# Row maxima of attention scores by a relu of a score difference: 22 tiles ahead of the loop, one tile in four inside it

## The chip, the cores and the metric

The program runs on 1 core of one Trainium2 chip. A core has a matrix engine (TensorE, PE in the rows; PEld is its weight load), a vector engine (VectorE, DVE), a scalar engine (ScalarE, ACT), GpSimd (POOL), a queue engine (SyncE, SP) and 16 DMA engines. Each engine works through its own list of instructions in order, and semaphores order the engines among each other. The metric is device time in microseconds (us), the median over runs; lower is better.

## The reference, cut to what matters

The program computes two layers on x of shape 2 x 1024 x 256: grouped attention with rotary positions, a feed-forward block with table-coded weights, a recurrent time-mix layer and a mixture of experts. The change touches the attention of the first layer:

```python
q = compute_rope((x @ W_Q.T).reshape(2, 1024, 16, 16))     # 16 heads of 16 numbers
k = compute_rope((x @ W_K.T).reshape(2, 1024, 16, 8))      # 8 key heads, each for 2 query heads
scores = einsum('bsdkg,btdk->bkgst', q, k) / sqrt(256)
w = softmax(scores, axis=-1)
ctx = einsum('bkgst,btdk->bkgsd', w, v)
```

The softmax needs the maximum of each query row over its 1024 keys before the exponentials can be taken. Feed-forward weights are `lut[idx]`, sixteen table values looked up by index; that lookup is done by other engines while attention runs.

## The kernel before, in words

**Projection.** The first 55 us load x, normalize it, turn it, and compute q, k and v on PE for four blocks of 512 tokens. DVE applies the rotary positions (`rope`), ACT cuts the result into a high part (`cut`), POOL makes the low part (`low_parts`), and SP stores both to DRAM (`block_out`); from there `load_qk` brings them back as tiles QS and KS with 48 rows per head (three products of 16 numbers), the two query heads of a key head at partitions 0 and 64. The pair of batch and key head is called n (0 to 15).

**Row maxima.** For one n there are 16 tiles of 128 queries (8 query blocks, 2 heads g). For tile k PE makes two matmuls (`maximum(k, 0)` and `maximum(k, 1)`, line 765), each 128 queries by 512 keys into a bank of PSUM, and DVE reduces the 128 x 1024 scores to 128 maxima (`row_max`, line 695). Two pairs of banks take turns, so the matmul of tile k waits for the reduction of tile k-2 (`max_done`). After 16 tiles the maxima are turned (`turn_max`), split in two parts by POOL (`max_parts`), sent through DRAM and loaded as two more rows of QS (`place_max`), so that the score matmul subtracts them. The first 26 tiles (16 + AHEAD) are made ahead of the loop.

**The loop.** For each n there are 8 steps t. PE's list in a step is, in this order: the two matmuls of tile k (k = 26 + 16n + 2t); the scores S0 and S1 (line 781, 128 keys by 512 queries each); four matmuls with the values for step t-2 (`weigh`, line 793, each shown as two records); the scores S2 and S3; the two matmuls of tile k+1. Scores go to a ring of three banks, so a score waits until the exponential three places before it has left its bank (`p_ready`). ACT takes the exponentials E0 to E3 of a step in order (line 681), and once per n it copies the result out (line 563) between E2 and E3 of step 1. DVE's list in a step is the reductions of k and k+1, and in even steps a table lookup between them (line 720), whose products POOL adds (line 622). In the last rounds the lookups come closer together.

The order is written out by hand in the functions `attend_tensor`, `attend_scalar`, `attend_vector`, `attend_gpsimd` and `attend_sync`; nothing is scheduled by a tool.

## Time and profile before

| | |
|---|---|
| device time, median of 3 runs | 884.34 us (880.03 to 892.65) |
| span of the profiled execution | 864.7 us |
| median less the span | 19.6 us (lowest run less the span: 15.3) |
| PE busy | 780.4 us, 90% |
| DVE busy | 694.2 us, 80% |
| ACT busy | 524.5 us, 61% |
| POOL busy | 363.9 us, 42% |

The busy times are sums over the whole program, whose stages have different limits; what the change is worth has to be read from the two stages it touches: about 56 to 89 us (tiles ahead of the loop) and 89 to 438 us (the loop). The pace of a stage shows in the distance of starts in the timeline, and what bounds it in the wait that ends last.

### The profile page before, as it was taken

The numbers are of one execution on the slowest core, as the hardware profiler recorded it, in microseconds if no ns is written. First come the engines' busy times: TensorE is split into PE (matmuls) and PEld (weight loads), VectorE is DVE, ScalarE is ACT, GpSimd is POOL, SyncE is SP. The second block draws the span as 40 slices with busy tenths as digits, with TensorE's granted clock in tenths as the row PEclk, the third lists the DMA queues.
The fourth block names the chain that finished last, engine by engine and source line by source line (L and its number), as shares of the span: only waits on it lengthen the run. The fifth ranks groups of instructions, "written<-read, shape, count | busy, mean of one in ns | idle before, by whom it ended". The sixth has DMA issues, their size and how long they took to land. (4 is left out here: it accounts for less than half of the span.)

```text
span 864.7 us, 17911 instructions
## 1 busy us (share of the span) xinstructions
PE 780.4 (90%) x6593; PEld 503.9 (58%) x6593; DVE 694.2 (80%) x1094; ACT 524.5 (61%) x965; POOL 363.9 (42%) x296
## 2 busy tenths in 40 slices
PE   3999999999999999998999999899575989999996
PEld 2863333333333333332368888798465887999875
DVE  5789999999999999996137666567899877666586
ACT  4520688888788888886864333543757653666442
POOL 6430255535753575359410001003698680444340
PEclk9985799999999999997999999999587989999999
DMA  6497022222222222200029000000104423344352
GB/s 240 174 225 290 2 46 54 52 52 52 52 53 52 52 52 52 56 16 13 20 85 250 2 1 0 14 1 13 60 5 150 174 93 60 117 131 127 115 160 74
DMA packets 59510, 69.97 MB, mean 81 GB/s; under 512 B 24768, under 2 KB 46400, under 8 KB 59040
## 3 DMA queue, kind: packets, MB, share of 16 engines
q1 hardware_dynamic: 55272, 58.30, 24.9%
q0 software_dynamic: 3408, 9.38, 3.1%
q10 hardware_dynamic: 744, 1.15, 0.4%
q8 instruction: 54, 0.88, 0.4%
q14 instruction: 32, 0.26, 0.1%
HBM read 40.07 MB, written 26.62 MB: 77 GB/s over the span
## 5 line engine op out<-in xcount | busy, mean ns | idle before, releaser
L681 ACT ACTIVATE probs_t<-psum 128x512 f32<-128x512 f32 x512 | 271.6, 601 | 98.7 <-PE psum L781 96.7
L695 DVE TENSOR_REDUCE row_max<-psum 128x1 f32<-128x1024 f32 x256 | 297.7, 1213 | 6.2 <-PE psum L765 5.9
L622 POOL TENSOR_TENSOR lut_sum<-lut_sum,lut_tmp 128x1080 f32<-128x1080 f32 x60 | 151.8, 2530 | 160.6 <-DVE lut_tmp L720 159.9
L765 PE MATMUL psum<-KS,QS 48*128 48x512 f32 x512 | 188.7, 470 | 19.6 <-DVE row_max L695 18.6
L781 PE MATMUL psum<-QS,KS 50*128 50x512 f32 x512 | 194.7, 471 | 1.0 <-ACT probs_t L681 1.0
L781 PEld LDWEIGHTS psum<-QS,KS 50*128 50x128 f32 x512 | 82.9, 189 | 135.3 <-ACT probs_t L681 124.7
L793 PE MATMUL psum<-probs_t,VS 128*32 128x512 f32 x1024 | 139.1, 616 | 1.0
L765 PEld LDWEIGHTS psum<-KS,QS 48*128 48x128 f32 x512 | 81.3, 199 | 76.1 <-DVE row_max L695 70.9
L2420 POOL DMA_INDIRECT y_rows<-y_slot,ids x39 | 37.5, 961 | 62.4 <-ACT y_slot L2483 62.1
L720 DVE TENSOR_SCALAR lut_tmp<-lut_idx,lut 128x1080 f32<-128x1080 int32 x60 | 48.7, 813 | 10.2 <-POOL lut_sum L622 10.2
L1179 POOL TENSOR_TENSOR rstd<-var_eps,minus_half 128x4 f32<-128x4 f32 x8 | 8.4, 1044 | 100.5 <-DVE var_eps L1174 100.5
L793 PEld LDWEIGHTS psum<-probs_t,VS 128*32 128x32 f32 x1024 | 20.8, 108 | 37.1 <-ACT probs_t L681 24.8
L1277 POOL TENSOR_TENSOR key<-key,tot 128x512 f32<-128x512 f32 x24 | 29.6, 1251 | 9.5 <-PE psum L2184 7.3
L450 PE MATMUL psum<-xTh,ffn_l 128*128 128x512 f32 (+1 forms) x80 | 31.5, 394 | 1.4 <-DVE f_h L1039 1.4
L452 PE MATMUL psum<-xTh,ffn_h 128*128 128x512 f32 (+1 forms) x80 | 31.5, 393 | 0.0
L451 PE MATMUL psum<-xTl,ffn_h 128*128 128x512 f32 (+1 forms) x80 | 31.5, 393 | 0.0
L984 ACT ACTIVATE f_silu<-psum 128x512 f32<-128x512 f32 (+1 forms) x24 | 14.3, 597 | 27.9 <-PE psum L452 27.9
L2579 DVE TENSOR_TENSOR xt_l<-psum,xt_h 128x256 fp32r<-128x256 f32 x39 | 16.5, 424 | 17.6 <-ACT xt_h L2490 17.5
L991 ACT ACTIVATE f_hh<-f_h 128x512 fp32r<-128x512 f32 (+1 forms) x24 | 15.2, 631 | 23.8 <-DVE f_h L1039 23.0
L1039 DVE TENSOR_TENSOR f_h<-psum,f_silu 128x512 f32<-128x512 f32 (+1 forms) x24 | 16.5, 687 | 16.0 <-ACT f_silu L984 15.6
L2483 ACT ACTIVATE y_slot<-psum,w_tile 128x256 f32<-128x256 f32 x39 | 18.6, 476 | 16.6 <-PE psum L2736 16.6
L2184 PE MATMUL psum<-recept,key 128*32 128x64 f32 x1024 | 21.0, 244 | 7.6 <-issue 4.5
(322 smaller groups left out, 1801.9 us busy)
## 6 DMA issues: line engine op xcount, KB each, us to landing
KS<-k_rows SPq DMA_DIRECT2D x31, 192.0 KB, 4.6
QS<-q_rows SPq DMA_DIRECT2D x31, 192.0 KB, 4.9
x_rows<-zero_rows SPq DMA_DIRECT2D x1, 4992.0 KB, 17.8
x_slot<-x_rows SPq DMA_DIRECT2D x39, 128.0 KB, 2.2
m_raw<-experts_w SPq DMA_DIRECT2D x2, 2432.0 KB, 13.3
q_rows<-part SPq DMA_DIRECT2D x8, 512.0 KB, 8.7
y_token<-y_rows SPq DMA_DIRECT2D x8, 512.0 KB, 7.6
x_tok<-x SPq DMA_DIRECT2D x4, 512.0 KB, 7.4
```

The source lines that it names most:

```text
L450: nc.tensor.matmul(out, ll, rh, start=start and i == 0, stop=False)
L451: nc.tensor.matmul(out, lh, rl, start=False, stop=False)
L452: mm = nc.tensor.matmul(out, lh, rh, start=False, stop=stop and i == n - 1)
L622: nc.gpsimd.tensor_tensor(wsum[:, c % 2, :], wsum[:, c % 2, :], wtmp[:, slot % 2, :], ALU.add).then_inc(lut_add, 1)
L681: nc.scalar.activation(pt[:, k % NPT, :], ring(k)[:], ACT.Exp, scale=float(E) ** -0.5).then_inc(p_ready, 1)
L695: nc.vector.tensor_reduce(mx[:, n % 2, col:col + 1], m.psum[:, 2 * (k % 2):2 * (k % 2) + 2, :], AX_XY, ALU.max).then_inc(max_done, 1)
L720: nc.vector.tensor_scalar(wsum[:, c % 2, :] if v == 0 else wtmp[:, slot % 2, :], idx[:, cols], float(v), lut[:, v:v + 1], ALU.is_equal, AL ...
L765: mm = nc.tensor.matmul(MX[k % 2][h][:], QS[n % NQK][rows(g, NROW), st * P:(st + 1) * P], KS[n % NQK][rows(g, NROW), h * BLK:(h + 1) * BLK ...
L781: nc.tensor.matmul(ring(k)[:], KS[n % NQK][rows(g, NAUG), t * P:(t + 1) * P], QS[n % NQK][rows(g, NAUG), half * BLK:(half + 1) * BLK], sta ...
L793: nc.tensor.matmul(OB[32 * j:32 * (j + 1), :], m.VS[:, bb * NTT + t, kv, :], pt[:, k % NPT, :], start=(t == 0), stop=(t == NTT - 1)).then_ ...
L1277: nc.gpsimd.tensor_tensor(k[:, :, 0, :], k[:, :, 0, :], t[:, :, 1].unsqueeze(2).broadcast_to([P, S // (2 * s), s]), ALU.mult).then_inc(k_d ...
L2420: nc.gpsimd.indirect_dma_start(m.y_rows, bass.IndirectOffsetOnAxis(ap=ids[:, j:j + 1], axis=0), yo[:, j % 4, :], None).then_inc(ys_out[j % ...
```

## The change

For keys in two halves, max(a, b) = relu(a - b) + b. A tile by the new way is: PE makes the score *difference* (queries against the difference of the two halves of the keys, tile KD) into the first bank and the scores of the second half into the second bank; ACT takes the relu of the first bank to SBUF (128 x 512); DVE does one `tensor_tensor_reduce` over 128 x 512: relu plus second bank, reduced by max. ACT's relu waits for both matmuls of the tile (`max_ps`).

- Ahead of the loop: tiles 0 to 3 as before, tiles 4 to 25 (22 tiles) the new way; all eight banks serve as four pairs, so a matmul waits for the reduction four tiles back.
- In the loop: tiles with k % 4 == 3 from 27 to 255 (58 tiles) the new way. These are tile k+1 of the even steps. ACT's relu stands between E1 and E2 of that step. Two pairs of banks, as before.
- The key difference: POOL subtracts the halves (`difference`), ACT and POOL split it, SP stores it to DRAM (`kd_rows`), and `load_diff` loads it per n, on ACT's queue for n = 0, else on SP's.
- SP's list at the start is in another order: the difference goes out ahead of the loads of QS and KS; the stores of the second half of q and k, and the load for n = 3, now follow behind `place_max(0)`, which has moved from ACT's queue to SP's; the first table index load comes earlier, the second at n = 1.
- Tiles for table sums and lookups have other addresses, and the sum is kept whole.

```diff
+    def difference(pool, bb):
+        pool.wait_ge(rot_ready, 6 * bb + 6)
+        if bb >= 1:
+            pool.wait_ge(kd_out, 32 * bb)
+        nc.gpsimd.tensor_tensor(kd[:], krot[0][:], krot[1][:], ALU.subtract).then_inc(kd_ready, 1)
...
         take_xt(3)
+        difference_high(act, 0)
...
         cut(act, 2)
+        act.wait_ge(kd_out, 32)
+        m.load_diff(act, 0)
         take_v(act, 2)
...
+    FIRST, PLAIN = NST + AHEAD, 4
+    def pair(k):
+        return 2 * (k % 4) if k < FIRST else 2 * (k % 2)
+    def by_relu(k):
+        return PLAIN <= k < FIRST or k % 4 == 3 and k >= FIRST
...
+    def part_above(act, k):
+        act.wait_ge(max_ps, k + 1)
+        if k == PLAIN:
+            act.wait_ge(m.prod_k, 2 * NB)
+        nc.scalar.activation(relus[k % 4 if k < FIRST else 0][:], bank[pair(k)], ACT.Relu).then_inc(relu_done, 1)

     def attend_scalar(act):
         m.project_scalar(act)
-        place_max(act, 0)
+        for k in range(PLAIN, FIRST):
+            part_above(act, k)
+            if k == NST - 1:
+                m.difference_high(act, 1)
...
                 nc.scalar.activation(pt[:, k % NPT, :], ring(k)[:], ACT.Exp,
                                      scale=float(E) ** -0.5).then_inc(p_ready, 1)
+                unit = (n + 1) * NST + AHEAD + G * (i // NJ) + 1
+                if i % NJ == 1 and unit < NG * NST and by_relu(unit):
+                    part_above(act, unit)
...
+            out, j = mx[:, n % 2, col:col + 1], pair(k)
+            if by_relu(k):
+                dve.wait_ge(relu_done, relu_number(k) + 1)
+                above = relus[k % 4 if k < FIRST else 0]
+                nc.vector.tensor_tensor_reduce(above[:], bank[j + 1], above[:], 1.0, LOWEST, ALU.add, ALU.max,
+                                               out).then_inc(max_done, 1)
+            else:
+                nc.vector.tensor_reduce(out, m.psum[:, j:j + 2, :], AX_XY, ALU.max).then_inc(max_done, 1)
...
-            if k >= 2 and h == 0:
-                pe.wait_ge(max_done, k - 1)
+            back = 4 if k < FIRST else 2
+            if k >= back and h == 0:
+                pe.wait_ge(max_done, k - back + 1)
```

SP's list in the change, from the first store of the difference:

```diff
         sp.wait_ge(m.ones_ready, NQK)
+        m.difference_out(sp, 0)
         load_qk(sp, 0, (0,))
-        for n in range(1, NQK):
-            load_qk(sp, n)
-        for tb in range(NB // 2, NB):
-            m.block_out(sp, tb)
...
+        load_qk(sp, 1)
+        sp.wait_ge(m.kd_out, 32)
+        load_diff(sp, 1)
+        load_qk(sp, 2)
...
+        load_diff(sp, 2)
+        place_max(sp, 0)
+        m.difference_out(sp, 1)
+        load_qk(sp, NQK - 1)
+        for tb in range(NB // 2, NB):
+            m.block_out(sp, tb)
         for n in range(NG):
+            if n == 0:
+                place_max(sp, 1)
```

How the instructions stand. ACT's list where the loop begins, before: line 580 and 584 place the first maxima, line 681 is the exponentials, line 563 the copy of the result.

```order
L580 DMA m_rows<-max_parts 16x2x32 x3
L584 DMA QS_72<-m_rows 2x1024 [waits mp_out]
L584 DMA QS_72<-m_rows 2x1024
L681 ACTIVATE probs_t<-psum 128x512 [waits s_ps] x10
L681 ACTIVATE probs_t<-psum 128x512 [waits pv_done,s_ps] x29
L563 ACTIVATE o_sb<-psum 128x512 [waits pv_done]
```

The same place in the change: line 766 is the relu, line 791 the exponentials, line 647 the copy.

```order
L766 ACTIVATE relu_108<-psum 128x512 [waits max_ps]
L766 ACTIVATE relu_109<-psum 128x512 [waits max_ps]
L791 ACTIVATE probs_t<-psum 128x512 [waits s_ps] x2
L766 ACTIVATE relu_108<-psum 128x512 [waits max_ps]
L791 ACTIVATE probs_t<-psum 128x512 [waits s_ps] x8
L766 ACTIVATE relu_108<-psum 128x512 [waits max_ps]
L791 ACTIVATE probs_t<-psum 128x512 [waits pv_done,s_ps] x8
L766 ACTIVATE relu_108<-psum 128x512 [waits max_ps]
L791 ACTIVATE probs_t<-psum 128x512 [waits pv_done,s_ps] x8
```

The relu has come in after two exponentials (E0, E1 of an even step) and then after every eighth; E2 and E3 of that step stand behind it.

PE's list in the change over a step and a half of n = 0: line 909 is the scores, line 921 the matmuls with the values, line 897 those for the maxima; KD2 is the key difference for n = 2.

```order
L909 MATMUL psum<-QS0_72,KS0_76 128x512 [waits p_ready] x2
L921 MATMUL psum<-probs_t_87,VS_55 32x512 [waits p_ready] x4
L909 MATMUL psum<-QS0_72,KS0_76 128x512 [waits p_ready] x2
L897 MATMUL psum<-KD2_105,QS2_74 128x512 [waits kd_in2,max_done]
L897 MATMUL psum<-KS2_78,QS2_74 128x512
L897 MATMUL psum<-KS2_78,QS2_74 128x512 [waits max_done]
L897 MATMUL psum<-KS2_78,QS2_74 128x512
L909 MATMUL psum<-QS0_72,KS0_76 128x512 [waits p_ready] x2
```

The places are those of before (there line 765 with KS stood where KD2 stands now): the matmuls whose result the relu takes come behind S2 and S3 of the step, and S0 and S1 of the next step behind the matmuls of the next tile.

DVE's list in the change, where the lookups in the loop begin: line 813 is the new reduction, one instruction over 128 x 512 and one that writes the 128 maxima; line 816 the old one, line 843 the lookup.

```order
L816 TENSOR_REDUCE row_max<-psum 128x1 [waits max_ps]
L843 TENSOR_SCALAR lut_sum<-lut_idx,lut 128x1080 [waits max_done,idx_in,lut_in]
L813 ISA relu_108,row_max<-psum,relu_108 128x512 [waits relu_done,max_ps]
L813 ISA row_max 128x1
L816 TENSOR_REDUCE row_max<-psum 128x1 [waits max_ps] x3
L843 TENSOR_SCALAR lut_tmp<-lut_idx,lut 128x1080 [waits kd_out]
L813 ISA relu_108,row_max<-psum,relu_108 128x512 [waits relu_done,max_ps]
L813 ISA row_max 128x1
```

Per two steps DVE has three old reductions, one new one (as two instructions) and one lookup; before it had four old ones and the lookup.

## Rows read from the trace of the kernel before

**Rows 1.** The page: costliest groups (count, busy us, mean ns, idle before and releaser).

```profile
L681 ACT ACTIVATE probs_t<-psum 128x512 f32<-128x512 f32 x512 | 271.6, 601 | 98.7 <-PE psum L781 96.7
L695 DVE TENSOR_REDUCE row_max<-psum 128x1 f32<-128x1024 f32 x256 | 297.7, 1213 | 6.2 <-PE psum L765 5.9
...
L720 DVE TENSOR_SCALAR lut_tmp<-lut_idx,lut 128x1080 f32<-128x1080 int32 x60 | 48.7, 813 | 10.2 <-POOL lut_sum L622 10.2
```

**Rows 2.** Windows: start:end length, busy PE, PEld, DVE, ACT, POOL, PEclk, DMA share, GB/s.

```profile
88.90:437.80 348.90, 330.95 (x2008) 118.23 (x2011) 315.61 (x325) 281.31 (x533) 180.26 (x112) 0.97 0.20 42
393.60:409.30 15.70, 13.65 (x60) 4.18 (x56) 9.97 (x12) 8.77 (x17) 13.64 (x9) 0.67 0.06 13
59.60:75.00 15.40, 14.13 (x25) 6.05 (x25) 14.33 (x14) 0.00 (x0) 0.89 (x1) 0.50 1.02 346
```

**Rows 3.** Timeline, PE held up behind a lookup: start, duration, engine, line, idle and releaser.

```profile
303.70 0.50 PE L765 MATMUL psum<-KS,QS 48*128 48x512 f32 x1 [0.29 <-DVE row_max L695]
```

**Rows 4.** Timeline, the loop step after that one (PE and ACT).

```profile
305.43 0.49 PE L781 MATMUL psum<-QS,KS 50*128 50x512 f32 x1
...
305.77 0.69 PE L765 MATMUL psum<-KS,QS 48*128 48x512 f32 x2
...
305.96 2.06 ACT L681 ACTIVATE probs_t<-psum 128x512 f32<-128x512 f32 x4 [0.37 <-PE psum L781]
...
306.61 0.50 PE L781 MATMUL psum<-QS,KS 50*128 50x512 f32 x1
...
308.04 0.49 PE L781 MATMUL psum<-QS,KS 50*128 50x512 f32 x1
```

**Rows 5.** Timeline, steps with no maxima; the second one holds the copy of the result.

```profile
417.15 0.50 PE L781 MATMUL psum<-QS,KS 50*128 50x512 f32 x2
...
419.76 0.50 PE L781 MATMUL psum<-QS,KS 50*128 50x512 f32 x2
...
420.79 0.59 ACT L563 ACTIVATE o_sb<-psum 128x512 f32<-128x512 f32 x1
...
422.52 0.50 PE L781 MATMUL psum<-QS,KS 50*128 50x512 f32 x2
```

**Rows 6.** Timeline in the projection and at the first tiles: DVE, POOL, SP's queue.

```profile
38.75 3.80 POOL L242 TENSOR_TENSOR part<-rotated,part 128x512 fp32r<-128x512 f32 x3 [5.25 <-ACT part L229]
...
40.23 1.29 DVE L370 TENSOR_TENSOR xTl<-psum,xTh 128x512 fp32r<-128x512 f32 x2 [2.07 <-ACT xTh L294]
...
46.38 0.33 SPq L190 DMA_DIRECT2D KS<-k_rows  x1
...
56.12 4.61 DVE L695 TENSOR_REDUCE row_max<-psum 128x1 f32<-128x1024 f32 x4 [2.28 <-PE psum L765]
```

**Rows 7.** Timeline, the last tiles ahead of the loop and the first exponentials.

```profile
85.06 2.35 PE L765 MATMUL psum<-KS,QS 48*128 48x512 f32 x4 [0.18 <-DVE row_max L695]
...
87.59 0.79 PE L765 MATMUL psum<-KS,QS 48*128 48x512 f32 x1 [0.18 <-DVE row_max L695]
...
88.88 2.08 ACT L681 ACTIVATE probs_t<-psum 128x512 f32<-128x512 f32 x4 [31.15 <-PE psum L781]
```

**Rows 8.** DMA issues from 30 to 110 us: count, KB each, median us to landing.

```profile
KS<-k_rows SPq DMA_DIRECT2D x7, 192.0 KB, 8.2
```

**Rows 9.** Timeline at 391 us: who takes a tile as soon as its matmuls end.

```profile
390.99 0.49 PE L781 MATMUL psum<-QS,KS 50*128 50x512 f32 x1
...
391.51 2.06 ACT L681 ACTIVATE probs_t<-psum 128x512 f32<-128x512 f32 x4 [0.37 <-PE psum L781]
...
391.79 1.23 DVE L695 TENSOR_REDUCE row_max<-psum 128x1 f32<-128x1024 f32 x1 [0.33 <-PE psum L765]
```

**Rows 10.** Timeline, a long wait in the loop and the steps behind it.

```profile
396.11 0.49 PE L765 MATMUL psum<-KS,QS 48*128 48x512 f32 x1 [1.79 <-DVE row_max L695]
...
402.12 1.22 PE L781 MATMUL psum<-QS,KS 50*128 50x512 f32 x3
...
406.18 0.79 PE L781 MATMUL psum<-QS,KS 50*128 50x512 f32 x2
```

More of the change, by code:

```diff
@@ L348, in project_gpsimd @@
         nc.gpsimd.memset(m.KS[NQK - 1][:].bitcast(F32), 1.0).then_inc(ones_ready, 1)
-        for tb in range(NB):
-            low_parts(pool, tb)
+        for bb in range(B):
+            for tb in (2 * bb, 2 * bb + 1):
+                low_parts(pool, tb)
+            difference(pool, bb)
+            difference_low(pool, bb)
     def project_vector(dve):
@@ L503, in attention_stage @@
     mres_done = sem("mres_done")
+    relu_done = m.front_sem("relu_done")
+    kd_in = [m.front_sem(f"kd_in{i}") for i in range(4)]
     gu_ps = m.gu_ps = sem("gu_ps")
@@ L758, in maximum @@
                 pe.wait_ge(qk_in[n % NQK], 16 * m.LOADS * (n // NQK + 1))
[L759 to L760 removed]
+            back = 4 if k < FIRST else 2
+            if k >= back and h == 0:
+                pe.wait_ge(max_done, k - back + 1)
             if k == 1 and h == 0:
                 pe.wait_ge(m.v_out, NT)
+            if k == 2 and h == 0:
+                pe.wait_ge(m.prod_q, 4 * NB)
+                pe.wait_ge(m.prod_k, 2 * NB)
             st, g = divmod(i, G)
[L765 to L766 removed]
+            keys = KS[n % NQK][rows(g, NROW), h * BLK:(h + 1) * BLK]
+            if by_relu(k) and h == 0:
+                q = diff_tile(n)
+                pe.wait_ge(kd_in[q], 32 if n < 2 else 16 * (n // 2))
+                keys = KD[q][rows(g, NROW), :]
+            mm = nc.tensor.matmul(bank[pair(k) + h], QS[n % NQK][rows(g, NROW), st * P:(st + 1) * P], keys,
+                                  start=True, stop=True)
             if h == 1:
@@ L817, in up_two @@
                 mm.then_inc(gu_ps, 1)
-        for k in range(NST + AHEAD):
+        for k in range(FIRST):
             maximum(k, 0)
@@ L1193, in norm @@
                                     ALU.subtract, ALU.mult).then_inc(m.xb_ready, 1)
+LOWEST = -3.4028234663852886e38
 LH, LD = 4, 64
```

110 lines of the change are left out of this document (80 added, 30 removed).

## The prediction

> **What bounds the kernel now.** I read the page's groups first. DVE spends 297.7 us on 256 reductions of 1.21 us, and ACT, with 512 exponentials, idles 98.7 us, nearly all of it waiting for PE's scores [rows 1]. The windows show where: over the loop (348.9 us for 128 steps, so 2.73 us a step) DVE is busy 315.6, ACT 281.3 and PE 331 us; ahead of it, at 59.6 to 75 us, DVE is busy 14.3 of 15.4 us, ACT not at all, and PE runs at a granted clock of 0.50, its 1.2 GHz level [rows 2].
>
> The timeline then shows that two different things bound the loop. In a step with a lookup before it PE waits 0.29 us for DVE's reduction [rows 3]. The next step has no such wait and still takes 2.61 us, because it is a closed chain between PE and ACT [rows 4]. Call T the start of S2 (305.43). Its exponential E2 starts at T+0.53; the next step's S1, which needs the bank that E2 leaves, at T+1.18; behind S1 come the matmuls with the values, and the next S2 at T+2.61. A step with no maxima at all, 417.15 to 419.76, takes 2.61 us too [rows 5]. So 2.61 us is the floor, whatever DVE does: 128 x 2.61 = 334.1 us, and only 348.9 - 334.1 = 14.8 us of the loop lie above it.
>
> ACT does idle, 0.37 us ahead of E2 in this step [rows 4], but that gap lies ahead of S2's result, and E2 is on the chain.
>
> **The change, part by part.**
>
> *DVE per new tile.* The nearest row for the 128 x 512 pass is a difference of a PSUM and an SBUF operand, two in 1.29 us; one old pass is a quarter of 4.61, 1.15 [rows 6]. The new pass is then at least 0.60 (two overlap a little) and, with the small instruction that writes the maxima behind it, at most that of two whole passes, 1.29. I take 0.73, near the low end, since the second instruction has one number a row.
>
> *Tiles ahead of the loop.* Two tiles now take 2.53 us (85.06 to 87.59), 1.27 each, with PE waiting 0.18 us for DVE [rows 7]. With four pairs of banks that wait goes. PE's own need: neighbouring tiles stand on different rows of the array, so they can run side by side, as S3 and the maxima do in the loop [rows 4]; at the slow clock, where one matmul takes up to 0.79 us [rows 7], a tile then costs PE 0.6 to 0.8 us. ACT's relu is 0.50 (the exponentials' pace, four in 2.06 [rows 4]), and ACT was idle here [rows 2]. So DVE sets the pace: 22 x (1.27 - 0.73) = 11.9 us less. What can eat it is a late key difference. POOL's low part for block 1 ends at 42.55; the difference (1.27, a third of 3.80), ACT's cut and the low part end at about 45.7; SP turns to loads at 46.4 [rows 6]. Store and load at up to 8.2 us each [rows 8] give 63 at the latest, and 58 at three quarters of that; tile 4 comes up at 56.12 + 4.61 = 60.7 [rows 6]. I allow 1.1 us. Front: **-10.8 us**, bounds -13 and -3. The first exponential comes at about 78.1 in place of 88.88 [rows 7].
>
> *The relu in the loop*, 58 tiles. It takes the matmuls of tile k+1, which stand behind S2 and S3 in PE's list. In the twin of this moment S2 starts at 390.99 and E2 at 391.51, and DVE, which was idle and waited for just these matmuls, starts at 391.79, T+0.80 [rows 9]. The relu can start no sooner, and E2 stands behind it in ACT's list. E2 starts at T + 0.80 + 0.50 = T+1.30 in place of T+0.53: 0.77 us later, and S1, the matmuls with the values and the next S2 move with it, since nothing in the chain has slack. The next step is at its floor and catches nothing up. So an even step is 3.38, an odd one 2.61, and 58 x 0.77 = **+44.7 us**. Bounds: 0.50 a tile (the relu alone, if its matmuls were in when S2 ends) and 0.90, so 29 to 52. E3, the next E0 and E1 follow at 0.5 us each and end at about T+3.4, just in time.
>
> *What DVE gives back.* Per two steps it needs 3 x 1.15 + 0.73 + a lookup of 0.81 [rows 1] = 5.0 us, against 5.99 of the new pair. So PE's waits for reductions go. Of the 14.8 us above the floor, the copy of the result keeps its 0.15 (2.76 for 2.61 [rows 5]) in 15 rounds, 2.3 us. A wait of 1.79 us and slow steps behind it [rows 10] make four steps last 15.7 us [rows 2] where 10.4 is the floor: 5.3 us, of which I leave half, since the lookups of the last rounds stay as dense. 0.4 is the loop's first steps. So 14.8 - 2.3 - 2.7 - 0.4 = 9.4: **-9.4 us**, bounds -6 and -12.
>
> *At nothing.* The second difference is made while tiles run. SP's stores of the second half now follow the first maxima (sent at about 71 us) and must be issued before the second ones are sent; 12 stores and 6 other transfers at about 1 us each end at 90, and the second maxima are needed at the loop's second round, 78 + 8 x 3 = 102. The cover is a dozen microseconds less two trips of some 4; if it is gone it costs up to 5 us, once. The difference loads, one per round on SP, are issued rounds ahead; POOL's subtractions, three more, fall in its idle time.
>
> The sum: 44.7 - 9.4 - 10.8 = +24.5. On the profiled execution that is a span of 864.7 + 24.5 = 889 us; the runs' median lies 19.6 above that span (the lowest 15.3), which I carry over: 884.3 + 24.5, rounded to **908 us**.
>
> *A rule against the trace.* ACT is idle for all of 59.6 to 75 us [rows 2], so a relu there takes nothing from anyone, while in the loop it lengthens the chain. The Trainium skill, page "ScalarE: Activation LUTs", section "Rules for kernel authors", says to give relu to VectorE, not to ScalarE. By that rule the new tiles would cost DVE one pass more, 22 x (0.60 + 0.73 - 1.27) = +1.3 us ahead of the loop in place of -11.9. The trace speaks against the rule there.
>
> **The rivals.**
>
> *The relu is hidden (faster).* ACT idles 0.37 us ahead of E2 [rows 4], three quarters of a relu. If the matmuls of tile k+1 were done before S2's result, the relu would fit in that gap, and the loop would drop towards its floor: -9.4 - 10.8 = -20, **864 us**. It decides where a relu costs under 0.05 us. Against it stand PE's order and the start at 391.79 [rows 9]. Chance 0.13.
>
> *It costs, but little.* 0.25 us a tile, half the relu: 14.5 - 20.2 = -6, **878 us**, nothing to be measured. Chance 0.12.
>
> *The forecast.* Chance 0.63, own range 896 to 921.
>
> *The start stalls or the new pass is dear.* If the difference lands 5 us late, if the second maxima wait behind SP's stores, or if the new pass takes 1.2, front and start give 0 to 4 in place of 10.8: **917 us**. Chance 0.07.
>
> *The clock falls.* PE was at 0.50 ahead of the loop [rows 2], with waits of 0.18 us between tiles [rows 7], and behind the wait of 1.79 us; steps then take 4.06 us (402.12 to 406.18) [rows 10]. A relu step adds 0.77 us in which PE has no work. Were a third of the steps slow, that adds 43 x 1.45 = 62 to the forecast, **970 us**. Against it: PE would still work 2.6 of 3.4 us, and waits of 0.29 us left the loop's clock at 0.97 [rows 2, 3]. The Trainium skill, page "TensorE: Matmul & The Clock Gate", section "What's actually happening", has the throttled state as the default and recent activity as what lifts it; this case is what that rule would do here if relu steps counted as idle. Chance 0.05.
>
> **How the numbers follow.** A measurement of this kernel can tell about 2% from no change, here 867 to 902. Faster: the hidden relu, 0.13, and the edge of the next case, together 0.14. Within 2%: the rest of the cheap relu, 0.11, and the forecast's low end (its bounds 29 - 12 - 13 reach +4), 0.10, together 0.21. Slower: 0.65. The range runs from 880, leaving out the hidden relu and part of the cheap one, to 922, leaving out the clock case: 0.20 in all.
>
> **What the changed profile would show.** First exponential at 76 to 80 us; 22 tiles at 0.65 to 0.80 us. In the loop, steps that alternate between about 3.4 and 2.6 us; ACT idle some 0.8 us ahead of each relu, released by PE's maxima; E2 right behind the relu, and the next S1 released by E2; DVE's busy share of the loop down from 0.90 to about 0.76. The forecast is wrong if relu steps stay under 3.0 us, if the relu starts before T+0.7, or if PE's granted clock in the loop leaves 0.9.

## The result, and the profile after

| | before | changed |
|---|---|---|
| device time, median | 882.88 us (880.03 to 892.65, 4 runs) | 908.70 us (906.41 to 911.59, 4 runs) |
| ratio to before | 1 | 1.0304 (95%: 1.0265 to 1.0342) |
| span of the profiled execution | 864.7 us | 904.6 us |
| first exponential | 88.88 us | 80.74 us |
| end of the attention (ScalarE loads its table for silu) | 437.76 us | 465.05 us |
| loop, between these two | 348.9 us | 384.3 us |

The change costs 3%: 25.8 us, where +24.5 was forecast. The loop grew by 35.4 us (44.7 - 9.4 = 35.3 forecast) and the front gave back 8.1 (10.8 forecast). Below, T is the start of S2 again; a relu step is one in which ScalarE has a relu, a plain step one without.

The page of the changed kernel first, in the columns of [rows 1]. L791 is the exponential, L816 the old reduction, L813 the new pass, L766 the relu, L897 the maxima matmuls, L909 the scores, L921 the values.

```profile
L791 ACT ACTIVATE probs_t<-psum 128x512 f32<-128x512 f32 x512 | 267.4, 606 | 37.8 <-PE psum L909 37.7
L816 DVE TENSOR_REDUCE row_max<-psum 128x1 f32<-128x1024 f32 x176 | 208.9, 1216 | 42.8 <-PE psum L897 42.8
...
L909 PE MATMUL psum<-QS,KS 50*128 50x512 f32 x512 | 193.7, 465 | 38.8 <-ACT probs_t L791 38.5
...
L766 ACT ACTIVATE relu<-psum 128x512 f32<-128x512 f32 x80 | 47.4, 597 | 50.9 <-PE psum L897 50.8
L813 DVE CUSTOM_DVE_ANT_0 relu<-psum,relu 128x512 f32<-128x512 f32 x80 | 54.0, 690 | 26.9 <-ACT relu L766 26.7
```

VectorE was relieved of what it was given too much of: 297.7 us of reductions [rows 1] are now 208.9 + 54.0, and it idles 42.8 us for TensorE's maxima where it idled 5.9. What is new is that TensorE waits 38.5 us for exponentials (L909; it was 1.0 us there in the kernel before), and that ScalarE waits 50.8 us with a relu at the head of its list. TensorE did gain by VectorE's free time, since its waits for a reduction in the loop fell from 15.1 us to 1.7, but it lost more to the exponentials.

The loop as a window (start:end length, busy PE, PEld, DVE, ACT, POOL, granted clock, DMA share, GB/s), to be set beside [rows 2]:

```profile
80.74:465.05 384.31, 343.60 (x2009) 126.08 (x2010) 294.50 (x383) 305.72 (x591) 179.42 (x112) 0.99 0.25 58
```

VectorE is busy 294.5 of 384.3 us, 0.77 of the loop (0.76 forecast), where it was 0.90; the granted clock is 0.99. Two steps of that loop in the timeline (start, duration, engine, line, idle and releaser), a relu step from 263.91 and the start of the plain one behind it:

```profile
263.91 0.50 PE L909 MATMUL psum<-QS,KS 50*128 50x512 f32 x1
263.92 0.50 PE L897 MATMUL psum<-KD,QS 48*128 48x512 f32 x1
...
264.72 0.60 ACT L766 ACTIVATE relu<-psum 128x512 f32<-128x512 f32 x1 [0.82 <-PE psum L897]
...
265.22 2.06 ACT L791 ACTIVATE probs_t<-psum 128x512 f32<-128x512 f32 x4
...
265.46 0.69 DVE L813 CUSTOM_DVE_ANT_0 relu<-psum,relu 128x512 f32<-128x512 f32 x1 [0.30 <-ACT relu L766]
265.86 0.50 PE L909 MATMUL psum<-QS,KS 50*128 50x512 f32 x1 [0.61 <-ACT probs_t L791]
...
266.29 1.07 PE L921 MATMUL psum<-probs_t,VS 128*32 128x512 f32 x8
267.28 0.50 PE L909 MATMUL psum<-QS,KS 50*128 50x512 f32 x1
...
269.89 0.50 PE L909 MATMUL psum<-QS,KS 50*128 50x512 f32 x1
```

The relu starts at T + 0.81, E2 at T + 1.31, the next S1 at T + 1.95, the values at T + 2.38, and the next S2 at T + 3.37. The plain step that follows takes 2.61 us (267.28 to 269.89). This is the closed chain of [rows 4] with 0.76 us put into it.

The front, with the difference late:

```profile
62.89 0.89 PE L897 MATMUL psum<-KD,QS 48*128 48x512 f32 x2 [5.76 <-DMA KD<-kd_rows]
...
64.87 0.69 DVE L813 CUSTOM_DVE_ANT_0 relu<-psum,relu 128x512 f32<-128x512 f32 x1 [4.43 <-ACT relu L766]
65.48 0.08 DVE L813 DVE_READ_ACCUMULATOR2_ANT row_max<- 128x1 f32 x1
65.48 0.69 DVE L813 CUSTOM_DVE_ANT_0 relu<-psum,relu 128x512 f32<-128x512 f32 x1
```

The new pass takes 0.69 us and the small read behind it 0.08, but passes start 0.61 us apart (64.87 to 65.48). VectorE stood still for 4.43 us ahead of the first of them, because TensorE waited 5.76 us for the key difference.

The span grew by 39.9 us and the medians by 25.8. Of the 14 us between the two, 12.6 lie behind the attention, where the change edits nothing; an experiment below takes this up.

### The profile page after: what moved, and what is told of

The parts are those of the page before. It is cut to its first block and busy times, and to the rows that moved or that the text cites. A ratio compares the mean times of both kernels' runs of the same rounds, so it can differ in the third digit from the quotient of the medians.

```text
span 904.6 us, 18267 instructions
## 1 busy us (share of the span) xinstructions
PE 784.7 (87%) x6593; PEld 511.8 (57%) x6593; DVE 660.3 (73%) x1174; ACT 562.3 (62%) x1047; POOL 374.1 (41%) x300
## 3 DMA queue, kind: packets, MB, share of 16 engines
q10 hardware_dynamic: 672, 1.31, 0.5%
## 5 line engine op out<-in xcount | busy, mean ns | idle before, releaser
L791 ACT ACTIVATE probs_t<-psum 128x512 f32<-128x512 f32 x512 | 267.4, 606 | 37.8 <-PE psum L909 37.7
L816 DVE TENSOR_REDUCE row_max<-psum 128x1 f32<-128x1024 f32 x176 | 208.9, 1216 | 42.8 <-PE psum L897 42.8
L909 PE MATMUL psum<-QS,KS 50*128 50x512 f32 x512 | 193.7, 465 | 38.8 <-ACT probs_t L791 38.5
L909 PEld LDWEIGHTS psum<-QS,KS 50*128 50x128 f32 x512 | 83.5, 186 | 200.3 <-ACT probs_t L791 192.0
L897 PE MATMUL psum<-KS,QS 48*128 48x512 f32 x432 | 140.1, 436 | 1.9 <-DVE row_max L813 0.9
L921 PE MATMUL psum<-probs_t,VS 128*32 128x512 f32 x1024 | 137.0, 608 | 1.1
L897 PEld LDWEIGHTS psum<-KS,QS 48*128 48x128 f32 x432 | 74.4, 195 | 24.3 <-DVE row_max L816 14.2
L766 ACT ACTIVATE relu<-psum 128x512 f32<-128x512 f32 x80 | 47.4, 597 | 50.9 <-PE psum L897 50.8
L813 DVE CUSTOM_DVE_ANT_0 relu<-psum,relu 128x512 f32<-128x512 f32 x80 | 54.0, 690 | 26.9 <-ACT relu L766 26.7
L897 PE MATMUL psum<-KD,QS 48*128 48x512 f32 x80 | 42.7, 577 | 6.3 <-DMA KD<-kd_rows 5.8
L921 PEld LDWEIGHTS psum<-probs_t,VS 128*32 128x32 f32 x1024 | 20.8, 108 | 33.7 <-issue 23.3
L1573 POOL DMA_INDIRECT x_rows<-x_early,slots x16 | 22.6, 1415 | 21.9 <-DVE tile_terms L1802 13.3
```

The costliest lines, as they stand in the source:

```text
L791: nc.scalar.activation(pt[:, k % NPT, :], ring(k)[:], ACT.Exp, scale=float(E) ** -0.5).then_inc(p_ready, 1)
L813: nc.vector.tensor_tensor_reduce(above[:], bank[j + 1], above[:], 1.0, LOWEST, ALU.add, ALU.max, out).then_inc(max_done, 1)
L816: nc.vector.tensor_reduce(out, m.psum[:, j:j + 2, :], AX_XY, ALU.max).then_inc(max_done, 1)
L897: mm = nc.tensor.matmul(bank[pair(k) + h], QS[n % NQK][rows(g, NROW), st * P:(st + 1) * P], keys, start=True, stop=True)
L909: nc.tensor.matmul(ring(k)[:], KS[n % NQK][rows(g, NAUG), t * P:(t + 1) * P], QS[n % NQK][rows(g, NAUG), half * BLK:(half + 1) * BLK], sta ...
L921: nc.tensor.matmul(OB[32 * j:32 * (j + 1), :], m.VS[:, bb * NTT + t, kv, :], pt[:, k % NPT, :], start=(t == 0), stop=(t == NTT - 1)).then_ ...
```

## The experiments

All of them beside the kernel before, which ran with medians of 881 to 886 us; each ratio is to the runs of the kernel before that stood beside it. "Loop" is from the first exponential to the end of the attention in the profiled execution, of which there is one for each kernel.

| kernel | median us | ratio to before (95%) | first exp. | loop us |
|---|---|---|---|---|
| before | 882.9 | 1 | 88.88 | 348.9 |
| changed | 908.7 | 1.0304 (1.0265 to 1.0342) | 80.74 | 384.3 |
| front_only | 869.2 | 0.9867 (0.9817 to 0.9918) | 80.45 | 347.6 |
| loop_only | 919.1 | 1.0411 (1.0359 to 1.0462) | 85.28 | 392.7 |
| moved (relu behind E3) | 901.9 | 1.0229 (1.0193 to 1.0264) | 81.83 | 377.9 |
| after_e2 (relu behind E2) | 877.8 | 0.9949 (0.9916 to 0.9982) | 80.80 | 355.0 |
| wait_first | 908.8 | 1.0302 (1.0258 to 1.0345) | 79.03 | 392.9 |
| kd_first | 893.0 | 1.0111 (1.0081 to 1.0141) | 80.43 | 368.7 |
| quarter_relu | 892.4 | 1.0103 (1.0072 to 1.0134) | 80.56 | 369.3 |
| relu_a | 944.0 | 1.0698 (1.0657 to 1.0740) | 80.65 | 429.7 |
| relu_a_lookup0 | 940.6 | 1.0661 (1.0612 to 1.0710) | 80.83 | 418.4 |
| relu_a_early | 870.0 | 0.9825 (0.9781 to 0.9868) | 81.12 | 341.8 |
| plain8 | 865.8 | 0.9796 (0.9765 to 0.9828) | 77.98 | 345.9 |

### The two halves of the change apart

The relu tiles ahead of the loop only:

```diff
     def by_relu(k):
-        return PLAIN <= k < FIRST or k % 4 == 3 and k >= FIRST
+        return PLAIN <= k < FIRST
```

> The changed kernel with the relu tiles ahead of the loop only (22 tiles); in the loop all tiles by the old reduction. Theory: the loop is as before (348.9 us), the tiles ahead of it keep what the trace of the change shows (first exponential at 80.7 in place of 88.9), so 882.9 - 8 = 875 us. Rival (the rest of the change, such as the other order on SP's queue or the difference's transfers, slows the loop too): 885 or more.

869.2 us, 1.3% under the kernel before. The relu tiles in the loop only:

```diff
-    FIRST, PLAIN = NST + AHEAD, 4
+    FIRST, PLAIN = NST + AHEAD, NST + AHEAD
...
-        m.load_diff(act, 0)
...
-        for k in range(PLAIN, FIRST):
-            part_above(act, k)
-            if k == NST - 1:
-                m.difference_high(act, 1)
+        m.difference_high(act, 1)
```

> The changed kernel with the relu tiles in the loop only (58 tiles); all 26 tiles ahead of the loop by the old reduction, with four pairs of banks. Theory: first exponential near 88 us, the loop at 384 us as in the change, 908.7 + 7 = 916 us. Rival (the loop's loss comes from how the loop starts, with the clock at 0.50 and the stores running beside it): under 908.

919.1 us. By the ratios, the front is worth -11.7 us and the loop costs +36.3; together +24.6, and the whole change costs +26.8. So the two halves add up, and the part ahead of the loop is a gain by itself: only the loop's relu loses. The theory named both within 6 us.

The front's gain is not all the relu's. The second kernel has the four pairs of banks and no relu ahead of the loop, and its first exponential stands at 85.28 already, 3.6 us under the kernel before: VectorE's waits of 0.18 us between tiles are gone, and its first tile is 0.8 us earlier (55.35 against 56.12). The relu gives the other 4.8 us (80.45 for 85.28). So a relu on ScalarE is a gain while ScalarE is idle. The Trainium skill, page "ScalarE: Activation LUTs", section "Rules for kernel authors", says to give relu to VectorE. The trace does not agree in this stage, where ScalarE was not busy at all [rows 2]: by that rule the front would be 1.3 us longer, by the estimate of the prediction, and no run had the relu on VectorE.

The loop of the second kernel is 8.3 us longer in its profile than the changed kernel's with the same work, mostly because its clock fell twice. From 211 to 218 us and from 409 to 422 us the granted clock is 0.50, and nothing longer than a gap of 0.94 us stands ahead of either:

```profile
408.06 0.50 PE L905 MATMUL psum<-QS,KS 50*128 50x512 f32 x1 [0.94 <-ACT probs_t L787]
```

In the changed kernel a gap of the same 0.94 us (at 205.66) left the clock at 1.00.

### Where the relu stands in ScalarE's list

The price was said to come from the relu's place ahead of E2. So it was moved behind E3, off the chain:

```diff
-                if i % NJ == 1 and unit < NG * NST and by_relu(unit):
+                if i % NJ == 3 and unit < NG * NST and by_relu(unit):
```

> The changed kernel with one thing moved: the relu stands behind E3 of an even step, not between E1 and E2. Same work on every engine. Theory (the relu lengthens the closed chain S2, E2, next S1, values, because it stands ahead of E2): behind E3 it is off that chain, every step with maxima falls to the floor of 2.61 us, the loop from 384.3 us to about 340, the time to 908.7 - 44 = 865 us, some 18 below the kernel before. Rival (the relu costs by ACT's total work, or the new reductions and transfers slow the loop): the steps with a relu stay above 3.1 us and the time above 895.

901.9 us, not 865. The theory of the chain alone fell. The relu step did come down to its floor, but the step behind it now takes the delay. Timeline of two steps of this kernel (relu in the first):

```profile
263.04 0.69 DVE L813 CUSTOM_DVE_ANT_0 relu<-psum,relu 128x512 f32<-128x512 f32 x1 [1.01 <-ACT relu L766]
...
263.39 0.73 PE L909 MATMUL psum<-QS,KS 50*128 50x512 f32 x2
...
263.66 3.48 DVE L816 TENSOR_REDUCE row_max<-psum 128x1 f32<-128x1024 f32 x3
...
264.93 0.50 PE L897 MATMUL psum<-KS,QS 48*128 48x512 f32 x1 [0.41 <-DVE row_max L816]
...
266.59 0.49 PE L909 MATMUL psum<-QS,KS 50*128 50x512 f32 x1
```

The step behind the relu's takes 3.20 us (263.39 to 266.59). VectorE waits 1.01 us for the relu, its plain reductions come that much later, and the maxima matmul that needs the bank of the first of them stands ahead of the scores in TensorE's list. A relu tile is a path TensorE - ScalarE - VectorE - TensorE, and it can be late on either side. If the relu is early it stands ahead of an exponential that the chain waits for; if it is late VectorE is late. Between the two lies the place behind E2, which had been left out:

```diff
-                if i % NJ == 1 and unit < NG * NST and by_relu(unit):
+                if i % NJ == 2 and unit < NG * NST and by_relu(unit):
```

> One edit to the changed kernel: in the loop the relu stands between a step's third and fourth exponential (E2 and E3), no longer between the second and the third; the front is as changed. Theory A (the closed chain S2 -> E2 -> S1' -> values -> S2' sets the step, 2.61 us, and a relu costs only what it adds to that chain): E2 starts 0.53 us after S2 again, the relu runs at S2 + 1.05 to 1.65, E3 ends at S2 + 2.2, ahead of the next S2 at 2.61; a relu step falls from 3.36 to 2.61 to 2.75 us, the loop from 384.3 to 334 to 350 us, the time to 860 to 878 us. Theory B (the relu makes VectorE late wherever it stands, as it did behind the fourth exponential, where the step after it was 3.40 us): its reduction starts 0.3 us later than in the changed kernel, and the two-step pair stays at 5.8 to 6.0 us; the time stays at 895 to 909 us.

877.8 us, 31 us under the changed kernel by one character, and 0.5% under the kernel before. It is the end of theory A's range, and the loop of 355.0 us lies above A's 350, so both theories hold a part. Its timeline, a relu step and the one behind it:

```profile
263.06 0.50 PE L909 MATMUL psum<-QS,KS 50*128 50x512 f32 x1
...
263.60 0.60 ACT L791 ACTIVATE probs_t<-psum 128x512 f32<-128x512 f32 x1 [0.20 <-PE psum L909]
...
264.09 0.59 ACT L766 ACTIVATE relu<-psum 128x512 f32<-128x512 f32 x1
...
264.82 0.69 DVE L813 CUSTOM_DVE_ANT_0 relu<-psum,relu 128x512 f32<-128x512 f32 x1 [0.57 <-ACT relu L766]
...
265.67 0.49 PE L909 MATMUL psum<-QS,KS 50*128 50x512 f32 x1
...
266.93 0.49 PE L897 MATMUL psum<-KS,QS 48*128 48x512 f32 x1 [0.48 <-DVE row_max L816]
...
268.59 0.50 PE L909 MATMUL psum<-QS,KS 50*128 50x512 f32 x1
```

E2 is back at T + 0.54 and the relu step at its floor of 2.61 us (263.06 to 265.67). The step behind it takes 2.92, with 0.48 us of it a wait for VectorE; it is the longest of the four plain steps of a round, most of the others take 2.71 to 2.78. Near the end of the loop a wait of 1.7 us for VectorE (at 392.6) and four slow steps behind it take some 6 us more than fast steps would, as in [rows 10]. Summed from 100 to 430 us (engine, waiting line, releaser: us in total, times, longest), the kernels with the relu behind E1, E2 and E3:

```profile
DVE relu L813 <- ACT relu L766: 19.0, 52, 1.0
...
PE psum L897 <- DVE row_max L816: 0.8, 2, 0.4
```

```profile
DVE relu L813 <- ACT relu L766: 30.2, 53, 1.3
...
PE psum L897 <- DVE row_max L816: 19.0, 54, 1.7
```

```profile
DVE relu L813 <- ACT relu L766: 56.4, 53, 2.2
...
PE psum L897 <- DVE row_max L816: 25.9, 55, 1.1
```

The later the relu, the more VectorE waits for it and TensorE for VectorE.

### What the 0.77 us of a relu step are made of

The forecast split them into 0.27 us of waiting for the tile's matmuls and 0.50 us of relu. The wait first: the relu needs only the first of the tile's two matmuls.

```diff
-        act.wait_ge(max_ps, k + 1)
+        act.wait_ge(diff_ps, relu_number(k) + 1)
...
+            if h == 0 and by_relu(k):
+                mm.then_inc(diff_ps, 1)
```

> The changed kernel, but the relu waits for the first of its tile's two matmuls only (a semaphore of its own); its place between E1 and E2 stays. Theory (0.77 us a tile is 0.28 of waiting for the second matmul and 0.49 of the relu itself): the first matmul ends with S2, at T+0.49, the relu starts at T+0.53, E2 at T+1.03; relu steps 3.11 in place of 3.36, 58 x 0.27 = 15 us off: 893. Rival (only the relu's own time counts and the wait is hidden): no change, 908.

908.8 us: nothing. (Its loop is longer in the table than the changed kernel's because its profile has stretches at a lower granted clock, 0.83 from 300 to 340 us, the fall standing behind a gap of 0.71 us; the medians are equal.) The relu still starts 0.80 us after S2. Its rows:

```profile
263.86 0.50 PE L912 MATMUL psum<-QS,KS 50*128 50x512 f32 x1
263.87 0.49 PE L898 MATMUL psum<-KD,QS 48*128 48x512 f32 x1
264.20 0.39 PE L912 MATMUL psum<-QS,KS 50*128 50x512 f32 x1
...
264.66 0.60 ACT L767 ACTIVATE relu<-psum 128x512 f32<-128x512 f32 x1 [0.81 <-PE psum L898]
```

The number is the rival's. But by its row, whose end is modelled, the difference's matmul ends at 264.36, and the relu starts at 264.66, 0.07 us after the end of S3 (264.20 + 0.39). S3 stands ahead of it in TensorE's list. So the next kernel also changed that order:

```diff
                 scores(n, t, 2)
+                maximum(k + 1, 0)
                 scores(n, t, 3)
-                for h in range(2):
-                    maximum(k + 1, h)
+                maximum(k + 1, 1)
```

> The kernel with the relu waiting for its first matmul alone gained nothing: the relu still started 0.80 us after S2. Here the difference's matmul is moreover issued between S2 and S3, not behind S3. If completions come in program order, so that the relu was held by S3 (start 0.34, length 0.39 after S2, then 0.07), the relu now starts at S2 + 0.54 and E2 at S2 + 1.05 in place of 1.30; 58 relu steps lose 0.25 us each, -14 us: 894 us. If something else holds the relu 0.8 us after S2 (for one the scalar engine's own passage from exponential to relu), nothing changes: 908 us.

893.0 us, where 894 was expected; the loop is 15.6 us shorter than the changed kernel's. A relu step of this kernel:

```profile
266.52 0.49 PE L912 MATMUL psum<-QS,KS 50*128 50x512 f32 x1
266.52 0.50 PE L898 MATMUL psum<-KD,QS 48*128 48x512 f32 x1
...
267.08 0.60 ACT L767 ACTIVATE relu<-psum 128x512 f32<-128x512 f32 x1 [0.57 <-PE psum L898]
...
269.64 0.50 PE L912 MATMUL psum<-QS,KS 50*128 50x512 f32 x1
```

The relu starts at T + 0.56, and the step takes 3.12 us, 0.25 less. That is the wait's share, so the wait was not hidden, as the rival had it, but stood behind S3. The Trainium skill, page "TensorE: Matmul & The Clock Gate", section "The mechanism" (under the packing of small matmuls), says that matmuls start and end in program order also where they run side by side. The release of the relu agrees with that; the recorded starts do not, since in the kernel before this one the difference's matmul has a start 0.33 us ahead of S3's.

The relu's own length, by a relu over 128 of 512 columns (this kernel leaves the other 384 columns as they were; the loop has 58 such tiles, the 80 of the expectation are all relu tiles of the program):

```diff
-        nc.scalar.activation(relus[k % 4 if k < FIRST else 0][:], bank[pair(k)], ACT.Relu).then_inc(relu_done, 1)
+        w = BLK if k < FIRST else BLK // 4
+        nc.scalar.activation(relus[k % 4 if k < FIRST else 0][:, 0:w], bank[pair(k)][:, 0:w], ACT.Relu).then_inc(relu_done, 1)
```

> In the loop's 80 relu tiles the relu reads and writes 128 of the 512 columns only, so that 384 columns of the maxima's term are stale; all else is as in the changed kernel. It takes the relu's own length away and leaves its wait. If the 0.77 us a relu step are a wait of 0.27 us and 0.50 us of the relu itself, the relu shrinks from 0.60 to about 0.25 us, a relu step from 3.36 to about 3.0 us, 58 steps save 20 us: 888 us, and relu steps remain 0.4 us over plain ones. If the wait for the maxima matmuls or VectorE were the price and not the relu's length, the time stays within 5 us of 908 us.

892.4 us, where 888 was expected. The relu takes 0.28 us in place of 0.60, and the loop is 15.0 us shorter, 0.26 us a relu step where the step of the timeline (263.11 to 266.16) has lost 0.31. So both parts are real: about a third of the 0.76 us is the wait behind S3, by the kernel with the other order, and two thirds are what is left for the relu's own time.

### The execution that the forecast was read from

> The kernel before, profiled once more. Its first profile has a span of 864.7 us under a median of 883 us, 18 us apart; the changed kernels' profiles lie 0 to 4 us from their medians, and each has a stretch in the time-mix stage in which TensorE issues in gaps and ScalarE's copy of kT waits 10 to 12 us. If the kernel before has that stretch in its usual executions too, a second profile shows it, with a span near 878 us, and the 12.6 us by which the changed kernel's profile is longer behind the attention are no effect of the change. If the stretch belongs to the changed kernels' code, this profile again shows kT copied four times within 17.3 us and a span near 865 us.

The span of this second profile of the kernel before is 882.3 us, 17.6 above the first. The relevant row (line, times: shortest, median, longest in ns, first and last start), of the first profile and of the second:

```profile
L1975 ACT ACTIVATE kT<-psum x4: 1024/1024/1026, 669.0 to 686.3; 128x1024 f32<-128x1024 f32 x4
```

```profile
L1975 ACT ACTIVATE kT<-psum x4: 1024/1024/1025, 675.8 to 705.7; 128x1024 f32<-128x1024 f32 x4
```

The four copies of kT, in a later stage, span 17.3 us in the first profile and 29.9 in the second, because of one wait of 14.3 us in the second that the first doesn't have. The changed kernel has it too (12.4 us; 696.5 to 727.2). Behind the attention the second profile takes 882.3 - 441.0 = 441.3 us, the changed kernel 439.5, the first profile 426.9. None of the kernel's timed runs took less than 878.9 us. So the first profile is an untypically short execution, and no effect of the change shows behind the attention. Against the second profile the end of the attention moves by 465.05 - 441.00 = 24.1 us, the medians by 25.8. What that wait is for is not shown.

In the loop the two profiles differ as well, by 4.2 us (348.9 and 353.1). The clock rises from 0.50 to 1.00 at 97.0 us in the first and at 109.0 us in the second, and three more steps of the second take 4.06 to 4.07 us.

### The relu on the other tile of the pair

If lateness of VectorE is all that is left in the kernel with the relu behind E2, a tile whose reduction comes later helps: k % 4 == 0, behind the plain reduction of tile 3, with the relu behind E3.

```diff
-        return PLAIN <= k < FIRST or k % 4 == 3 and k >= FIRST
+        return PLAIN <= k < FIRST or k % 4 == 0 and k >= FIRST
...
-        for g in range(G) if n < 2 else (1,):
+        for g in range(G) if n < 2 else (0,):
...
-                unit = (n + 1) * NST + AHEAD + G * (i // NJ) + 1
-                if i % NJ == 1 and unit < NG * NST and by_relu(unit):
+                unit = (n + 1) * NST + AHEAD + G * (i // NJ) + G
+                if i % NJ == 3 and unit < NG * NST and by_relu(unit):
...
-                if n < NG - 2 and i % 4 == 0:
+                if n < NG - 2 and i % 4 == 2:
```

> What is left of the relu's cost in the kernel with the relu behind E2 is VectorE's lateness: its new pass waits 0.5 us for the relu (32.5 us over the loop), the next maxima wait 0.3 to 0.5 us for VectorE, and two steps take 5.3 to 5.5 us in place of 5.22. Here the relu goes to the pair's other tile: k % 4 == 0 in place of 3, whose maxima matmuls end 0.3 to 0.4 us later than those of tile 3 but whose reduction comes after a plain one of 1.17 us. The relu stands behind E3 (S2 + 1.57 to 2.10), the new pass can start at S2 + 2.2 right behind the plain reduction (S2 + 0.8 to 2.0), and the lookup stands behind it, where VectorE would wait for the next maxima. If lateness is the whole rest: VectorE's wait for the relu falls under 15 us, two steps take 5.22 to 5.3 us, the loop 334 to 342 us against 348.9 before, the time 855 to 868 us, under both kernels and level with or under the kernel with relu tiles ahead of the loop only (869). If the relu's 0.52 us on ScalarE, which then has 2.6 us of work in a step of 2.61, is itself the bound (late E0 and E1 delay S2), two steps stay at 5.4 us or more and the time at 872 to 880 us.

944.0 us, the slowest of all and outside both expectations. The same with the lookup left where the changed kernel has it (without the last two lines of the diff):

> As the kernel with the relu on tiles k % 4 == 0 behind E3, but with the table lookup where the changed kernel has it, two reductions ahead of the new pass (behind tile 2). VectorE then does lookup 0.69 to 0.77, reduction 1.17, new pass 0.61, reduction, reduction. By the lateness theory the lookup pushes the reduction of tile 3 and with it the new pass later by up to 0.5 us, while VectorE idles behind the new pass until the next maxima; VectorE's sum is 4.97 us in 5.22, so at most 0.2 us of delay a pair stays: 0 to 12 us slower than with the lookup behind the new pass. If VectorE's order does not matter, the two are equal within 3 us.

940.6 us. The lookup's place decides nothing here, where something else rules; whether it matters without that was not tried. What rules, from the first of the two, in the waits from 80 to 530 us, in the timeline and in windows (length, busy PE, granted clock, DMA share, GB/s):

```profile
PE psum L897 <- DMA KD<-kd_rows: 49.5, 12, 4.9
```

```profile
133.99 0.43 SPq L592 DMA_DIRECT2D KD<-kd_rows  x1
136.28 0.76 PE L897 MATMUL psum<-KD,QS 48*128 48x512 f32 x1 [4.12 <-DMA KD<-kd_rows]
```

```profile
130.00:140.00 10.00, 5.80 (x29) 0.81 0.11 26
...
160.00:170.00 10.00, 6.13 (x28) 0.68 0.09 22
170.00:180.00 10.00, 10.00 (x44) 0.50 0.03 4
```

The first tile of a group is now a relu tile and needs the group's key difference three tiles, nearly two steps, earlier than before. SyncE issues that load only behind the stores of the head's output, which wait for that output. TensorE stands still for 4.1 us, in 12 of the 16 groups, 49.5 us in all. That is the larger part of the loss. The other is the clock: behind each pause the granted clock is 0.50, the 1.2 GHz level, for one to four steps, and a step wholly at that level takes 4.07 us (263.82 to 267.89) in place of 2.61. The loop is 87.9 us longer than with the load in time (the next kernel; the medians lie 74.0 apart, since the one was profiled in its slowest run and the other in its fastest); 87.9 - 49.5 = 38.4 us are left. Some 35 of them are in 27 steps of 3.3 to 4.07 us behind the pauses, the rest in the steps that hold the pauses. Gaps of 0.6 us in every relu step did not do this to the changed kernel (granted clock 0.99 in the loop), though the clock did fall with the relu in the same place in the kernel with the loop's relu only and in the one that waits for the first matmul. The Trainium skill, page "TensorE: Matmul & The Clock Gate", section "What's actually happening", has the throttled clock as the default that recent activity lifts; these windows agree.

The load was put at the head of SyncE's iteration:

```diff
         for n in range(NG):
+            if 2 <= n < NG - 2:
+                load_diff(sp, n + 2)
...
-            if 2 <= n < NG - 2:
-                load_diff(sp, n + 2)
             if 1 <= n < NG - 1:
                 place_max(sp, n + 1)
```

> As the kernel with the relu on tiles k % 4 == 0 behind E3 and the lookup behind the new pass, with one more edit: SyncE issues the load of the key differences for group n + 2 at the head of iteration n, ahead of the loads of Q and K and of the stores of the head's output, not behind them. In the kernel without it, TensorE waited for that load at 12 of 16 heads, 49.5 us in all (4.1 us each), and after each such pause its granted clock was 0.5 for some 10 to 20 us. If that wait is the whole of the 63 us loss, it goes, the clock stays at 1.00 through the loop, two steps take 5.22 to 5.3 us as they did between the pauses, the loop 334 to 345 us, and the time is 855 to 870 us (before 882, the kernel with relu tiles ahead of the loop only 869). If the clock falls in this order of work without any pause, the granted clock still shows stretches at 0.5 with no wait ahead of them, and the time is 900 us or more.

870.0 us, 1.8% under the kernel before, and 4.6% under the changed kernel by the ratios (0.9825 / 1.0304). The waits for the load are gone, and the slow clock behind them too:

```profile
100.00:200.00 100.00, 98.47 (x610) 38.59 (x608) 94.07 (x124) 92.17 (x178) 47.88 (x31) 1.00 0.32 68
```

```profile
DVE relu L813 <- ACT relu L766: 11.1, 39, 0.4
...
PE psum L897 <- DVE row_max L816: 1.7, 8, 0.4
```

TensorE is busy 98.5% of that window, VectorE waits 11.1 us for the relu in place of 30.2, and TensorE 1.7 us for VectorE. The loop is 341.8 us, 7 under the kernel before; 334.1 is the floor. With only the front changed it was 347.6. The medians of these two kernels do not tell them apart (their intervals overlap). In the traces the attention ends 5.1 us apart (422.94 and 428.08), but that is one execution each, and the second has a stretch at a clock of 0.50 (216 to 222 us). That the relu in the loop brings anything beyond the front's is not shown.

### Filling the wait for the key difference

Last, the term that the forecast had missed, on the best kernel so far:

```diff
-    FIRST, PLAIN = NST + AHEAD, 4
+    FIRST, PLAIN = NST + AHEAD, 8
```

> The best kernel so far (relu on tiles k % 4 == 0 behind E3, lookup behind the new pass, early load of the key differences) with eight plain tiles ahead of the relu tiles in place of four. In all kernels with relu tiles ahead of the loop TensorE waits 5.7 us for the key differences (until 62.9 to 63.3) and VectorE then 4.4 us for the relu; the first exponential came at 80.4 to 81.8 where 78.1 was forecast. Four more plain reductions (4 x 1.17 us, on VectorE from 60.9 on) fill that wait, and cost 4 x (1.17 - 0.67) = 2.0 us behind it: 4.4 - 2.0 = 2.4 us to be gained, the first exponential at 78.5 to 79, the time 866 to 869 us. If instead the key differences' landing itself moves (it is bound by its own transfer), VectorE's wait for the relu at this place stays above 3 us and nothing is gained: 870 us.

865.8 us, 2.0% under the kernel before. Its first tiles:

```profile
55.50 9.14 DVE L816 TENSOR_REDUCE row_max<-psum 128x1 f32<-128x1024 f32 x8 [2.35 <-PE psum L897]
...
62.61 0.89 PE L897 MATMUL psum<-KD,QS 48*128 48x512 f32 x2 [1.22 <-DMA KD<-kd_rows]
...
64.58 0.69 DVE L813 CUSTOM_DVE_ANT_0 relu<-psum,relu 128x512 f32<-128x512 f32 x1
```

VectorE goes from the last plain reduction straight to the new passes; the 4.4 us are gone. The first exponential stands at 77.98, 3.1 us earlier, of which 0.8 are an earlier first tile (55.50 against 56.26) and 2.4 what was expected. By the medians the gain is 4 us, and the intervals of the two ratios overlap. In the profiled executions nothing of the 3.1 us is left at the end of the attention (423.83 against 422.94), because the clock rises from 0.50 later, at 95.3 us and not at 90.4. In two profiles of the kernel before this moment lay 12 us apart, so it need not be the edit's doing.

## Why the prediction was right, step by step

- **The floor and the chain** (2.61 us, 334.1 us): held. A plain step that waits for nothing else takes 2.61 us in every kernel at the full clock, and the best loop reached is 341.8.
- **The relu step** (3.38 us, T + 0.80, T + 1.30): held, 3.37, T + 0.81, T + 1.31. That the relu stands on the chain is shown by the relu behind E2, with which the same step is 2.61 us. The split into wait and length is shown by kd_first and quarter_relu. The reason given for the start, that the relu takes the tile's matmuls as soon as they end, was right in the number and one step short: S3, which stands ahead of them, ends at the same moment.
- **What VectorE gives back** (-9.4): held as a sum, since the loop came out at 384.3 us against 348.9 + 35.3; with 58 x 0.76 = 44.1 us of relu, 6.1 us are left above the floor, where the forecast left 5.4. The long wait of [rows 10] at the end of the loop has no counterpart: the granted clock is 1.00 from 393.6 us to the end, where it was 0.67 around that wait [rows 2]. That the sum fits to 0.1 us is in part luck: against the second profile of the kernel before, whose clock rose later, the loop grew by 31.2 us.
- **The front** (-10.8, inside bounds of -13 to -3): right in kind, too large by 2.7 us. The pass was sized at 0.73 us and is 0.61 from start to start; with the ScalarE and TensorE work beside it a tile takes 0.68 (22 passes in 15.1 us, 65.25 to 80.31, in relu_a_early). That alone would give 22 x (1.27 - 0.68) = 13.0 us. The mis-sized term is the late key difference: 4.43 us of VectorE's time where 1.1 was allowed; 13.0 - 4.4 = 8.6 against the 8.1 measured. It landed at 62.9, the end of the range given (58 to 63), while the sum was made with the middle. From the last plain reduction (60.44) to the landing are 2.45 us; the other 1.98 are the tile's matmuls and its relu behind the landing (62.89 to 64.87), for which the forecast had no term. The first exponential, at 80.74, lies outside the 76 to 80 that it named.
- **The base** (the median lies 19.6 us above the profiled span, carried over): the number came out right, but it is no property of the kernel. The first profile was an untypical execution; in the changed kernel the profiled run's time is 906.4 us for a span of 904.6. With the difference added the sum is 908.8, which the text gives as 908. It was right to add the difference to the median, and the 889 us that the text gives for the span were nearly 16 too low.
- **At nothing**: SyncE's stores are hidden. The second maxima leave at 92.6 us and are placed at 100.24, where the text had 102 as the time they are needed, and no wait for them shows.
- **The rivals**: the hidden relu needs another place in the list and another tile, and then lands at 866 to 870 us. It was priced at 864 us. The clock case did not occur in the changed kernel, but it did in relu_a: 944 us, behind pauses of 4 us. The fear that relu steps alone could do it was not empty: with the relu in the same place, loop_only and wait_first have stretches of 7 to 13 us at 0.50 behind gaps of 0.94 and 0.71 us. They cost some 8 us of a loop, far from the 62 that the text priced, and what sets them off is not shown.

What the forecast did not see is that the same work can be had without the loss. It took the place between E1 and E2 as given and asked what it costs; its rival of a hidden relu needed the maxima done sooner, not another place.

## What to carry to other kernels

Work that moves from a full engine to one with idle time costs by its place in that engine's list, not by the idle time: here 0.76 us a tile ahead of an exponential that TensorE waits for, and a late VectorE one place too far behind. Follow the tile through all its engines, and give it to the tile, and the place, that has slack on both sides. When a consumer moves earlier, look at the queue that feeds it: a load that came in time for a tile nearly two steps later cost 50 us in waits and nearly 40 more in slow clock. Split a change that touches two stages and time the parts: one half of this one was a gain.

## What the runs showed of the hardware

- Of two matmuls that run side by side on different rows of the array, the later in the list releases its waiter no sooner than the earlier: a relu started 0.07 us after the end of S3 and not after its own producer, which by its record had ended 0.23 us before that (both ends are modelled). Putting the producer ahead of S3 released it 0.24 us sooner.
- Each of twelve pauses of TensorE of about 4 us was followed by one to four steps at a granted clock of 0.50. Gaps of 0.6 us every six microseconds left it at 0.99 in the changed kernel; behind a gap of 0.94 us it fell in one kernel (408.06) and not in another (205.66).
- In two executions of the same kernel the clock rose from 0.50 to 1.00 at 97.0 and at 109.0 us; the first steps of the second took 4.4 us longer.
- A tensor_tensor_reduce of 128 x 512 with one operand in PSUM is recorded as a pass of 0.69 us and a read of 0.08, and one starts every 0.61 us.
